# The feed-forward's last product in plain fp32: one gelu a block, no rounded halves

## What is computed

```python
x = _layernorm(x + attn(x))            # scan over the tokens, 16 heads of 8
# the feed-forward: w has the values -8, 0 and 8, s is a scale for each output
h = silu(_tlin(x, w1_w, w1_s)) * _tlin(x, w2_w, w2_s)   # 128 -> 512
h = gelu(_tlin(h, h1_w, h1_s))                          # 512 -> 512
h = gelu(_tlin(h, h2_w, h2_s))                          # 512 -> 512
y = _tlin(h, w3_w, w3_s)                                # 512 -> 128
x = _layernorm(x + y)
```

## Time and profile before

| | us |
|---|---|
| median of 3 runs | 193.92 (193.89 to 194.09) |
| the profiled execution | 193.71 |
| its span | 191.9 |
| TensorE busy | 162.0 |
| VectorE busy | 147.9 |
| ScalarE busy | 117.5 |
| GpSimd busy | 113.8 |

### The profile page before, as it was taken

One profiled execution on the slowest core, in us unless ns is written; L12 is line 12 of the kernel. 1 busy time (PEld: TensorE's weight loads), 2 busy tenths in 40 slices (PEclk: granted clock), 3 DMA queues, 4 the chain that ended last, 5 costly groups with the idle time before them and its releaser, 6 DMA issues.

```text
span 191.9 us, 2751 instructions
## 1 busy us (share of the span) xinstructions
PE 162.0 (84%) x790; PEld 124.0 (65%) x790; DVE 147.9 (77%) x301; ACT 117.5 (61%) x188; POOL 113.8 (59%) x94
## 2 busy tenths in 40 slices
PE   1859988969499997999999699999987999799840
PEld 1638656849387774878768487677856866567630
DVE  1398886988788997998999997899999685512360
ACT  4633649898037725378682556768454688979623
POOL 8989589919706689580677688427782313470011
PEclk9999999999979999999999999999999999999996
DMA  3999700000000000000000010000000100002002
GB/s 119 332 419 405 274 3 0 0 0 3 0 3 0 0 2 0 3 2 0 0 0 0 0 41 14 0 0 0 3 0 0 56 0 0 0 0 60 0 3 58
DMA packets 6191, 8.65 MB, mean 45 GB/s; under 512 B 513, under 2 KB 5026, under 8 KB 5666
## 3 DMA queue, kind: packets, MB, share of 16 engines
q1 hardware_dynamic: 5602, 5.60, 9.1%
q0 software_dynamic: 576, 2.88, 3.9%
HBM read 7.43 MB, written 1.05 MB: 44 GB/s over the span
## 4 chain that ended last, share of the span: by engine, by line
PE 25%; DVE 18%; issue 8%; ACT 5%; POOL 4%; DVEq 1%; POOLq 0%; ACTq 0%
PE ffn L600 8%; PE ffn L591 8%; DVE state L994 5%; DVE y L1005 2%; DVE y L1009 2%; DVE f_lo L1091 1%; ACT f_hi L831 1%; PE ffn L569 1%; DVE o_acc L1012 1%; DVE ffn L1080 1%; PE att L526 1%; POOL u_tok L313 1%; PE ffn L574 1%; ACT f_hi L839 1%; POOL o_rstd L332 1%
## 5 line engine op out<-in xcount | busy, mean ns | idle before, releaser
L354 POOL TENSOR_TENSOR f_lo<-full,f_hi 128x512 fp32r<-128x512 f32 x20 | 26.0, 1315 | 30.4 <-DVE full L1080 19.5
L994 DVE TENSOR_TENSOR_SCAN state<-gate,att 128x512 f32<-128x512 f32 x32 | 38.4, 1210 | 3.0 <-PE att L515 3.0
L839 ACT ACTIVATE f_hi<-ffn,vec_cols 128x512 fp32r<-128x512 f32 x32 | 22.1, 690 | 27.4 <-PE ffn L600 27.2
L591 PE MATMUL ffn<-f_hi,h_hi 128*128 128x512 f32 x128 | 36.7, 405 | 1.7 <-ACT f_hi L831 1.3
L600 PE MATMUL ffn<-f_lo,h_hi 128*128 128x512 f32 x128 | 35.6, 399 | 0.0
L591 PEld LDWEIGHTS ffn<-f_hi,h_hi 128*128 128x128 f32 x128 | 23.5, 188 | 8.7 <-ACT f_hi L831 3.0
L1091 DVE TENSOR_TENSOR f_lo<-ffn,f_hi 128x512 fp32r<-128x512 f32 x28 | 18.9, 687 | 12.4 <-ACT ffn L842 11.4
L600 PEld LDWEIGHTS ffn<-f_lo,h_hi 128*128 128x128 f32 x128 | 23.9, 188 | 5.8 <-DVE f_lo L1091 0.4
L313 POOL TENSOR_TENSOR u_tok<-kv_tok 128x1024 f32<-128x1024 f32 (+1 forms) x12 | 27.3, 2282 | 0.5 <-issue 0.4
L328 POOL TENSOR_TENSOR o_acc<-o_acc,y 128x512 f32<-128x512 f32 x16 | 20.6, 1290 | 7.9 <-DVE y L1005 7.8
L1005 DVE TENSOR_TENSOR y<-att,state 128x512 f32<-128x512 f32 x32 | 21.1, 671 | 0.0
(11 more groups left out here) (162 smaller groups left out, 318.6 us busy)
## 6 DMA issues: line engine op xcount, KB each, us to landing
h_raw<-in_hT SPq DMA_DIRECT2D x2, 1024.0 KB, 11.3
h_hi<-in_hT POOLq DMA_DIRECT2D x2, 1024.0 KB, 11.7
x_tok<-in_x SPq DMA_DIRECT2D x4, 256.0 KB, 5.0
out<-out_tok SPq DMA_DIRECT2D x3, 256.0 KB, 2.3
w_raw<-in_w12T SPq DMA_DIRECT2D x1, 512.0 KB, 4.6
w_hi<-in_w12T POOLq DMA_DIRECT2D x1, 512.0 KB, 8.1
xT_raw<-in_xT SPq DMA_DIRECT2D x1, 256.0 KB, 2.6
proj_raw<-in_proj SPq DMA_DIRECT2D x2, 128.0 KB, 2.3
```

Source lines behind the costliest of these rows:

```text
L354: nc.gpsimd.tensor_tensor(lo[:, o], full_block(layer, o), hi[:, o].bitcast(F32), ALU.subtract).then_inc(pool_rested, 1)
L591: nc.tensor.matmul(bank[:], h_hi[:, layer - 1, c, tile(o)], src_hi[:, c], start=(c == 0), stop=False)
L839: nc.scalar.activation(hidden[layer][0][:, o], bank[:], ACT.Gelu, scale=scales[:, 1 + layer, o:o + 1]).then_inc(gelu_hi_ready, 1)
L994: nc.vector.tensor_tensor_scan(state[:, k % 3], gate[:, b], A[2 + k % 2][:], 0.0, ALU.mult, ALU.add).then_inc(scanned, 1)
```

## The change

Layer 2's blocks are no longer split. ScalarE makes one gelu of each, in plain fp32, into a new tensor `f3` that lies where `f1_hi` lies. W3 is kept as one fp32 tensor `w3`, and `ffn_out` has four fp32 matmuls of 512 columns where eight fp32r ones stood. All four stand ahead of `transpose_x2`; nothing stands behind it. `last_out` has four fp32 matmuls of 256 columns a half. The remainders of layer 2 on VectorE, the second gelus, the rounded load of W3, its low half and its sum go, and TensorE waits for w3's load ahead of the branch.

```diff
-            def ffn_out_hi(b, with_lo):
-                bank_read(b, 2, 0)
+            def ffn_out(b):
                 for c in range(OB):
                     pe.wait_ge(gelu_hi_ready, 2 * OB * b + OB + c + 1)
-                    nc.tensor.matmul(W3_BANK[:], w3_hi[:, c], f1_hi[:, c], start=(c == 0), stop=False)
-                    if with_lo:
-                        nc.tensor.matmul(W3_BANK[:], w3_lo[:, c], f1_hi[:, c], start=False, stop=False)
-
-            def ffn_out_rest(b):
-                for c in range(OB):
-                    pe.wait_ge(*rested(b, 2, c))
-                    last = nc.tensor.matmul(W3_BANK[:], w3_hi[:, c], f1_lo[:, c], start=False, stop=(c == OB - 1))
+                    last = nc.tensor.matmul(W3_BANK[:], w3[:, c], f3[:, c], start=(c == 0), stop=(c == OB - 1))
                 last.then_inc(w3_ready, 1)
...
                     for c in range(OB):
                         pe.wait_ge(gelu_hi_ready, 2 * OB * b + OB + c + 1)
-                        nc.tensor.matmul(LAST_W3[h][:, half], w3_hi[:, c], f1_hi[:, c, half], start=(c == 0), stop=False)
-                        if with_lo:
-                            nc.tensor.matmul(LAST_W3[h][:, half], w3_lo[:, c], f1_hi[:, c, half], start=False, stop=False)
-                    for c in range(OB):
-                        pe.wait_ge(*rested(b, 2, c))
-                        last = nc.tensor.matmul(LAST_W3[h][:, half], w3_hi[:, c], f1_lo[:, c, half], start=False,
+                        last = nc.tensor.matmul(LAST_W3[h][:, half], w3[:, c], f3[:, c, half], start=(c == 0),
                                                 stop=(c == OB - 1))
...
-                ffn_out_hi(f, with_lo)
+                ffn_out(f)
                 transpose_x2(a)
-                ffn_out_rest(f)
                 first_layer(a, f, with_lo, follows)
...
+            pe.wait_ge(w3_loaded, 16)
             with pe.If(exact):
...
-                nc.scalar.activation(hidden[layer][0][:, o], bank[:], ACT.Gelu,
-                                     scale=scales[:, 1 + layer, o:o + 1]).then_inc(gelu_hi_ready, 1)
+                dst = f3[:, o] if layer == 2 else f2_hi[:, o]
+                nc.scalar.activation(dst, bank[:], ACT.Gelu, scale=scales[:, 1 + layer, o:o + 1]).then_inc(gelu_hi_ready, 1)
+                if layer == 2:
+                    return
...
             pool.dma_start(h_hi[:, 1], hT[:, 1]).then_inc(h2_hi_loaded, 16)
-            pool.dma_start(w3_hi[:], w3T).then_inc(w3_hi_loaded, 16)
...
             sum_over_k(0, (4, 5))
-            weight_lo(5)
             attention_end(0, (1, 2), True)
...
             silu_of_g(2)
-            sum_lo(5)
             silu_of_g(3)
...
                 add_x(a)
-                rest(f, 2, 0)
-                rest(f, 2, 1)
                 x2_normalise(a)
-                rest(f, 2, 2)
-                rest(f, 2, 3)
                 rest_of_x2(a)
```

More of the change, by code:

```diff
@@ L36, in gla_ffn_kernel @@
         ROW = L * 4
-        x_hi, x_lo, f1_hi, f1_lo = arena(
+        x_hi, x_lo, f1_hi, f1_lo, f3 = arena(
             "place_f1", 2 * B * ROW, ("x_hi", [P, B, L], F32R, 0), ("x_lo", [P, B, L], F32R, B * ROW),
-            ("f1_hi", [P, OB, L], F32R, 0), ("f1_lo", [P, OB, L], F32R, OB * ROW))
+            ("f1_hi", [P, OB, L], F32R, 0), ("f1_lo", [P, OB, L], F32R, OB * ROW), ("f3", [P, OB, L], F32, 0))
         h_raw, f2_hi, f2_lo = arena(
@@ L42, in gla_ffn_kernel @@
             ("f2_hi", [P, OB, L], F32R, 0), ("f2_lo", [P, OB, L], F32R, OB * ROW))
-        w12_raw, w3_raw, out_tok = arena(
-            "place_out", B * ROW, ("w12_raw", [P, 2, D_HID], F32, 0), ("w3_raw", [P, OB, HID], F32, 2 * ROW),
+        w12_raw, out_tok = arena(
+            "place_out", B * ROW, ("w12_raw", [P, 2, D_HID], F32, 0),
             ("out_tok", [P, B, TILES, HID], F32, 0))
@@ L66, in gla_ffn_kernel @@
         h_lo = sb("h_lo", [P, 2, OB, D_HID], F32R)
-        w3_hi = sb("w3_hi", [P, OB, HID], F32R)
-        w3_lo = sb("w3_lo", [P, OB, HID], F32R)
+        w3 = sb("w3", [P, OB, HID])
         ident = sb("ident", [P, P])
@@ L71, in gla_ffn_kernel @@
         rep = sb("rep", [P, DH, P], F32R)
-        lo_sums = sb("lo_sums", [P, 6])
-        lo_any = sb("lo_any", [P, 6])
+        lo_sums = sb("lo_sums", [P, 5])
+        lo_any = sb("lo_any", [P, 5])
         lo_flag = sb("lo_flag", [1, 1], mybir.dt.int32)
@@ L218, in gla_ffn_kernel @@
                                   flat(h_lo[:, n // 2, pair]), ((h1_loaded, h1_hi_loaded), (h2_loaded, h2_hi_loaded))[n // 2]))
-        weight_groups.append((flat(w3_raw[:]), flat(w3_hi[:]), flat(w3_lo[:]), (w3_loaded, w3_hi_loaded)))
         WG = len(weight_groups)
-        ALL_BLOCKS = [(layer, o) for layer in range(3) for o in range(OB)]
+        ALL_BLOCKS = [(layer, o) for layer in range(2) for o in range(OB)]
         ON_POOL = [(0, 0), (0, 1), (0, 2), (1, 0), (1, 1)]
         ON_DVE = [n for n in ALL_BLOCKS if n not in ON_POOL]
-        hidden = ((f1_hi, f1_lo), (f2_hi, f2_lo), (f1_hi, f1_lo))
+        hidden = ((f1_hi, f1_lo), (f2_hi, f2_lo))
         def rested(b, layer, o):
@@ L268, in _ @@
             sp.dma_start(h_raw[:, 1], hT[:, 1]).then_inc(h2_loaded, 16)
-            sp.dma_start(w3_raw[:], w3T).then_inc(w3_loaded, 16)
+            sp.dma_start(w3[:], w3T).then_inc(w3_loaded, 16)
             sp.dma_start(x_tok[:, 0], x_rows[0]).then_inc(x_loaded[0], 16)
@@ L351, in rest @@
                 else:
-                    pool.wait_ge(gelu_ready, 2 * OB * b + OB * (layer - 1) + o + 1)
+                    pool.wait_ge(gelu_ready, OB * b + o + 1)
                 hi, lo = hidden[layer]
@@ L550, in bank_read @@
                     pe.wait_ge(f1_ready, OB * b + o + 1)
+                elif layer == 2:
+                    pe.wait_ge(gelu_hi_ready, 2 * OB * b + OB + o + 1)
+                    return
                 else:
-                    pe.wait_ge(gelu_ready, 2 * OB * b + OB * (layer - 1) + o + 1)
+                    pe.wait_ge(gelu_ready, OB * b + o + 1)
                 if (layer, o) not in ON_POOL:
@@ L713, in rows @@
                         ffn_hidden_rest(B - 1, layer, o)
-                last_out(with_lo)
+                last_out()
             pe.wait_ge(gk_loaded, 48)
@@ L1088, in rest @@
                 else:
-                    dve.wait_ge(gelu_ready, 2 * OB * b + OB * (layer - 1) + o + 1)
+                    dve.wait_ge(gelu_ready, OB * b + o + 1)
                 hi, lo = hidden[layer]
@@ L1239, in _ @@
             last_row = B - 1
-            for layer in (1, 2):
-                for o in range(OB):
-                    rest(last_row, layer, o)
+            for o in range(OB):
+                rest(last_row, 1, o)
             for h in range(2):
```

4 lines of the change are left out of this document (2 added, 2 removed).

## The result

The changed kernel takes 198.78 us (median of 4 runs, 198.69 to 199.09), against 194.0 for the kernel before on the same chip. The ratio on record is 1.022, with an interval of 1.0144 to 1.0297; the medians alone give 1.025, since one of the four runs before took 196.31 us. The profiled execution took 198.85 us, with a span of 196.8. So the change costs 4.9 us of span, where 4.5 were forecast.

A forecast was written before the change was run, and what follows sets the result against it. TensorE bounds before each handover, VectorE from the scans on; what stands ahead of TensorE's x2 transposes is on the path. 1.83 + 0.81 + 2.13 - 0.1 - 0.2 + 0.05 = +4.5 us, giving 198.3 us, range 197.1 to 199.5.

The forecast's parts named there:

- The pass: W3 product on TensorE: each fp32 matmul is two passes of 0.427 us; eight take 3.41 us, the old product 1.87.
- Rival (e): W3 product: weight loads are not hidden, each pass pays one, 1.5 us more per handover and tail, 204.3 us; chance 0.02.
- The first and third handovers: Where row f's W3 product meets the next row's x2 transposes (84.9, 154.7 us): later by +1.83 and +2.13 us.
- The signs named beforehand: Profile after: x2 transposes end 4.0 us after the first pass; handover gaps about 1.5 and 1.1 us longer.
- The second handover: At 119.3 us: scans +0.81 us later; the old transposes were already late, waiting for normalised x2 (rstd on GpSimd).
- The tail: Last row, W3 product to transposes: 16 half-width passes take 3.42 us, two old waits go; -0.1 us.
- The start: Row 0: GpSimd's freed work readies o_acc 1.1 us sooner, but the beta projection waits for wout_beta; -0.2 us.
- The new wait for w3's load: TensorE ahead of the branch: the wait for w3_loaded costs a semaphore look, +0.05 us at most.
- The freed work: VectorE's four remainders (0.69 us) and ScalarE's four second gelus (0.66) a row: no path step waits for them.
- (b): Passes and restarts cost more: 0.16 us a product, first handover the whole 2.12; 199.1 us in total; chance 0.14.
- (c): The 23 us behind a handover absorb part, 0.7 us of the first two shifts lost; 196.9 us; chance 0.06.
- (d): Faster than before: passes at an fp32r matmul's 0.233 us give 192.3 us; turning point 0.28; chance 0.03.

The follow-up runs named there:

- e8: Changed kernel with four tiny VectorE instructions (128x1) in the third handover, where layer 2's remainders had stood; 198.71 us profiled, its other run 202.30.
- e6: Kernel before, with u_tok's first two groups of transposes moved ahead of the low half of the W3 product; 193.13 us, ratio 0.995.
- e3: Changed kernel with three second gelus and three subtractions a row put back beside the product for the first three rows, results unused; 198.1 us, ratio 1.0223.
- e2: Changed kernel with the W3 product's matmuls in the three handovers done twice, output unchanged; 209.72 us, ratio 1.0824.
- e1: Changed kernel with w3 and f3 rounded to fp32r, so each of the four W3 matmuls is one pass; 192.92 us, ratio to before 0.9897.
- e7: Changed kernel with the whole fp32 W3 product behind the transposes of x2, not ahead of them; 199.71 us, ratio 1.0301.

## Why the prediction was right

**The pass.** Forecast 0.427 us, measured 0.430; the product 3.41 and 3.43. The centring of o_acc was the right row to read, although it was only one fp32 product of 512 columns a row. Rival (e) is refuted: with a load of 0.190 us ahead of each, passes still start 0.430 apart, and those of 128 columns 0.111 apart, less than one load. The Trainium skill, "TensorE: Matmul & The Clock Gate", Part 3, "The mechanism", says that a weight load overlaps running matmuls only when the row group differs; this doesn't hold here. The same section also lets a load for the background weight buffer run ahead, which these figures would fit; the prediction left that out.

**The first and third handovers.** +1.83 and +2.13 forecast, +1.85 and +2.15 measured. Each step came out in its order: product, transposes, 0.12 to the rounding, x2_lo, scans. That the old wait of 0.29 us would vanish into the shift was right as well. The signs named beforehand came: the transposes end 4.03 us after the first pass, and the products start 36.12 and 36.13 us apart (85.03, 121.15, 157.28), 1.41 and 1.08 more than before. In the first handover two small errors of 0.08 cancel, which is luck: the product starts 30.38 us behind S0 and not 30.30, and the scans start 0.61 behind x2_lo's start, where the forecast gave x2_lo its whole 0.69.

**The second handover.** +0.81 forecast, +0.72 measured. The step that holds the first and failed the old one, r_rstd on GpSimd, is late again (the normalised x2 comes only from 121.94, 0.79 after the product's start), but the product is long enough to cover it. The 0.09 is nearly all the same 0.08 at x2_lo, which here nothing offsets.

**The tail** is the term that was mis-sized: -0.1 forecast, +0.24 measured. Timeline of the changed kernel's tail:

```profile
185.29 3.61 PE L614 MATMUL ffn<-f,w 128*128 128x256 f32 x16
185.49 0.69 ACT L825 ACTIVATE f<-ffn,vec_cols 128x512 f32<-128x512 f32 x1 [1.19 <-PE ffn L598]
...
188.74 0.38 PE L620 MATMUL att<-ident,yT 128*128 128x128 f32 x2
```

The part that the term was made for held: 185.29 to 188.74 is 3.45 us, against 3.52, which is -0.07. What was missed is ahead of it: from Y3 to the W3 product are 22.04 us and not 21.73, because of VectorE's late start of the last row's first layer. The step that failed is the sentence that VectorE's lost remainders cost or give nothing. e8 restores that start with four tiny instructions.

**The start.** -0.2 and +0.05 forecast. The projection of beta follows the pair sum's start by 3.81 us (42.06 - 38.25), and not 4.03: -0.22, by the reason given, since it waits for wout_beta. The new wait for w3's load shows in TensorE's idle time ahead of row 0's x2 transposes, before and after:

```profile
52.30 1.11 PE L545 MATMUL att<-ident,x 128*128 128x128 f32 x4 [2.68 <-issue]
...
52.60 0.79 PE L540 MATMUL att<-ident,x 128*128 128x128 f32 x4 [2.74 <-issue]
```

It is 2.68 and 2.69 us in the two kernels without that wait and 2.73 to 2.76 in the nine with it: +0.06, where the prediction had put +0.05 with no row for it. By these transposes, 10.5 us behind the projection, 0.13 of the gain is left. S0 itself moved by only 0.02, in a start that drifts by 0.9, so the sum can't test this term. The prediction's words that both load queues lose a load are wrong: SyncE's load of W3 stays, and only GpSimd's goes. No term hung on it. The contention was there and was read rightly: the pair sum took 1.82 us in the two profiles with `weight_lo(5)` (before and e6) and 0.69 in every kernel profiled without it. The Trainium skill, "SBUF — State Buffer", "Who interferes with whom", says that a VectorE instruction with two SBUF inputs contends with a GpSimd instruction that reads SBUF, and the trace agrees. What an instruction loses by it is not what the path loses: 1.13 us against 0.11 to 0.13 here.

**The freed work.** ScalarE's 11.5 and VectorE's 11.0 us gave nothing to the sum, and e3, which puts 12.1 of these 22.5 us back, costs nothing. For that part the reading that the work was under cover in the handovers is shown.

**The other rivals.** (b) asked for 0.02 more a pass and 2.12 us in the first handover; 0.003 and 1.85 were measured. (c) is refuted by e2. (d) needed passes of 0.28 us. No run has eight passes of that length, but e1, with half as many passes at the rate of an fp32r matmul, bears out its sign: with the same order it is faster than the kernel before.

The range (197.1 to 199.5) held the time, and the sum was right for its reasons: its three large terms agree to 0.1 us each, and e1, e2 and e7 bear them out. The total of +4.9 against +4.5 is the tail's 0.34 and the start's 0.13, less 0.05 in the handovers.

## What to carry to other kernels

The plain fp32 product was written with half as many matmuls as the split one, and took 3.43 us where 1.87 stood, since each fp32 matmul is two passes of 0.43 us, and an fp32r one starts every 0.233. Ask first of what engine the change takes time, and then what stands behind that engine's queue at the place. Work on engines that wait at the same spot is worth nothing there (12 us of it, put back, cost nothing); the order of TensorE's queue (8 transposes moved ahead of four matmuls, at two places) was worth 0.8 us with no work removed. Where executions drift in the start, compare stretches between fixed events, not totals: terms of 0.1 us could be read that way, where the granted clock in the stretch was the same.

## What the hardware showed beyond that

- In every execution profiled here TensorE's granted clock falls to the lower level (0.50, which is 1.2 GHz) for some us between 50 and 58 us, around the end of a stretch of 2.7 us in which TensorE does nothing, ahead of row 0's x2 transposes. In steps of 2 us from 52 us on it is 0.50, 0.65, 1.00 in the kernel before and 0.74, 0.50, 0.90 in the changed one; the full clock "in the middle of the run" holds from 58 us on. In e3 the low stretch is about twice as long (0.75 from 50 us, then 0.50, 0.50, 0.55), and costs 0.8 us.
- In e2's tail the clock fell to 0.57 for 4 us and cost 1.6 us far from the edit. Ahead of that TensorE was idle from 178 to 179 us and busy for 0.52 of the next. The changed kernel has such a gap too (busy 0.53 of the 2 us from 168) with no fall. No run tells the cases apart, or says why e3's fall is longer.
- VectorE began a product 0.46 us after the end of what it waits for, and 0.11 with four more tiny instructions ahead in its queue.
- A VectorE addition took 1.82 us beside GpSimd's outer product and 0.69 when it began as that product ended.
- Executions drift in the start: with the same code up to S0, S0 lay between 54.07 and 54.94 us.
